# Two small TensorE products in a kernel's head computed as row sums on POOL and ScalarE

## What is computed

```python
def L0(x, y, weight, mask, bias):                 # first layer
    masked_w = weight * mask[None]
    w_bot = einsum('bg,got->bot', y, masked_w)
    return einsum('bnt,bot->bno', x, w_bot) + bias

def L1(x, w, W_base, b_base, As, Bs):             # second layer, low-rank experts
    out = einsum('btc,oc->bto', x, W_base) + b_base
    h = einsum('btc,erc->bter', x, As)
    return out + einsum('bter,eor,be->bto', h, Bs, w) * 2.0

x = x + L0(x, cond_8, ...)
x = x + L1(x, cond_8, ...)
x = x + L2(x, cond_8, ...)                        # shared MLP and two of eight routed MLPs
x = x + L3(x, cond_8, ...)                        # one of eight gated MLPs, with biases
```

## Time and profile before

| What | Value |
|---|---|
| Runs | 134.33, 134.73, 135.54 us, median 134.73 |
| The profiled execution | 134.23 us, its span 132.4 us |
| Granted TensorE clock, mean | 0.997 of full speed |
| Busy share of PE, DVE, ACT, POOL | 97%, 75%, 75%, 57% |
| Instructions | 3286 |

### The profile page before, as it was taken

One profiled execution on the slowest core, in us unless ns is written; L12 is line 12 of the kernel. 1 busy time (PEld: TensorE's weight loads), 2 busy tenths in 40 slices (PEclk: granted clock), 3 DMA queues, 4 the chain that ended last, 5 costly groups with the idle time before them and its releaser, 6 DMA issues.

```text
span 132.4 us, 3286 instructions
## 1 busy us (share of the span) xinstructions
PE 128.1 (97%) x930; PEld 120.0 (91%) x930; DVE 98.8 (75%) x192; ACT 99.2 (75%) x206; POOL 75.8 (57%) x90
## 2 busy tenths in 40 slices
PE   7999999999999999999999999999999999999990
PEld 5978888888888999999999999999999999999980
DVE  0699898797776777767967777767768676898791
ACT  3784799979945569787797877766866769989860
POOL 0238459979970037468496785963542544426790
PEclk9999999999999999999999999999999999999998
DMA  4999999999005946566765657756577565664216
GB/s 134 358 398 409 407 401 400 400 403 392 29 0 240 372 184 247 228 239 246 317 272 222 249 228 304 298 226 249 220 288 313 228 254 226 273 272 186 82 44 198
DMA packets 11490, 34.56 MB, mean 261 GB/s; under 512 B 1104, under 2 KB 2512, under 8 KB 11472
## 3 DMA queue, kind: packets, MB, share of 16 engines
q1 hardware_dynamic: 11184, 34.15, 65.8%
q10 hardware_dynamic: 288, 0.20, 0.5%
HBM read 12.32 MB, written 1.05 MB: 101 GB/s over the span
## 4 chain that ended last, share of the span: by engine, by line
PE 89%; ACT 3%; POOL 1%; issue 1%; DVE 1%; ACTq 1%; DVEq 0%; POOLq 0%
PE up L298 30%; PE acc L298 30%; PE gate L298 29%; ACT h_pair L619 1%; DVE x_res L979 1%; POOL x_lo L762 1%; POOL x_res L788 1%; ACT h_pair L692 1%; ACT h_act L683 1%; ACTq L224 0%; ACT h_act L672 0%; DVE h_pair L1010 0%; ACT dn_hi L637 0%; ACT out_part L661 0%; POOL dn_lo L756 0%
## 5 line engine op out<-in xcount | busy, mean ns | idle before, releaser
L756 POOL TENSOR_TENSOR dn_lo<-slabs,dn_hi 128x256 fp32r<-128x256 f32 x40 | 29.7, 742 | 39.0 <-ACT dn_hi L637 38.9
L613 ACT ACTIVATE h_act<-gate 128x512 f32<-128x512 f32 x48 | 28.8, 600 | 23.2 <-PE gate L298 21.1
L907 DVE TENSOR_TENSOR h_pair<-up,h_pair 128x512 fp32r<-128x512 f32 x55 | 37.6, 684 | 0.0
L917 DVE SCALAR_TENSOR_TENSOR up<-h_act,w_route,up 128x512 f32<-128x512 f32 x32 | 24.2, 756 | 16.9 <-PE up L298 16.7
L298 PE MATMUL gate<-x_hi,w_gu 128*128 128x256 f32 x160 | 33.9, 276 | 0.0
L298 PE MATMUL up<-x_hi,w_gu 128*128 128x256 f32 x158 | 33.4, 276 | 0.0
L619 ACT ACTIVATE h_pair<-up 128x512 fp32r<-128x512 f32 x55 | 32.9, 598 | 0.0
L298 PEld LDWEIGHTS gate<-x_hi,w_gu 128*128 128x128 f32 x160 | 27.1, 188 | 0.2
L298 PEld LDWEIGHTS up<-x_hi,w_gu 128*128 128x128 f32 x158 | 26.8, 188 | 0.0
L298 PE MATMUL acc<-h_pair,dn_hi 128*128 128x256 f32 x140 | 25.6, 276 | 0.0
L298 PE MATMUL gate<-x_lo,w_gu 128*128 128x256 f32 x80 | 22.1, 276 | 0.0
(11 more groups left out here) (125 smaller groups left out, 201.4 us busy)
## 6 DMA issues: line engine op xcount, KB each, us to landing
w_gu<-slabs SPq DMA_DIRECT2D x40, 512.0 KB, 3.1
slabs<-slabs_moe SPq DMA_DIRECT2D x8, 768.0 KB, 12.7
slabs<-slabs_l SPq DMA_DIRECT2D x4, 768.0 KB, 9.3
sh_raw<-slabs_shared SPq DMA_DIRECT2D x2, 384.0 KB, 5.0
x_res<-x_rest SPq DMA_DIRECT2D x1, 768.0 KB, 6.6
outT<-x_res SPq DMA_DIRECT2D x6, 128.0 KB, 2.0
slabs<-second_in SPq DMA_DIRECT2D x1, 320.0 KB, 3.1
slabs<-third_in SPq DMA_DIRECT2D x1, 256.0 KB, 3.8
```

The source lines that it names most:

```text
L613: nc.scalar.activation(h_act[:, u % 2, :], gate_ps[u % 2][:], ACT.Gelu_apprx_tanh).then_inc(act_done, 1)
L756: nc.gpsimd.tensor_tensor(dn_lo[:, q % W_SLOTS, :], slab_cols(at, DOWN_AT, 256), dn_hi[:, q % W_SLOTS, :].bitcast(F32), ALU.subtract).then ...
L907: V.tensor_tensor(h_lo[:, u % H_SLOTS, :], h_of(u), h_hi[:, u % H_SLOTS, :].bitcast(F32), ALU.subtract).then_inc(h_lo_done, 1)
L917: ins = V.scalar_tensor_tensor(h_of(u), h_act[:, k, :], weight, h_of(u), ALU.mult, ALU.mult)
```

## The change

The products As bias_l0 and (W_base) bias_l0 are no longer computed on PE. POOL multiplies each matrix elementwise with a row that repeats bias_l0 on all partitions, and ACT sums each product along its rows with the accumulator output of an Identity. So `lora_aT` isn't loaded any more, and W_base is loaded a second time, untransposed, with the repeated row beside it: `fourth_in` has four blocks of 128 columns where it had three. The identity's part of the constant, bias_l0 itself, is added to bias_l1 on POOL. PE keeps one product for the constant, line 358. On DVE the scaling of the product moves behind the two masks of batches 2 to 7, and `c_b` takes two per-partition operands, and waits for both sums and for POOL's.

```diff
-        fourth_sb = early(3, P)
+        fourth_sb = early(4, P)
...
-        w_baseT, ident, lora_aT = (fourth_sb[:, k, :] for k in range(3))
+        w_baseT, ident, w_base, bias_row = (fourth_sb[:, k, :] for k in range(4))
...
+        bias_terms = early(2, P)
...
+        a_bias, base_bias, bias_sum = (sb(n, [P, 1]) for n in ("a_bias", "base_bias", "bias_sum"))
...
             pe.wait_ge(bw_ready, 1)
             lora(gate_ps[0][:, 0:S], 0, 2)
-            pe.wait_ge(d_fourth, DMA)
-            mm(acc_ps[:, 512:512 + B], lora_aT, bias_l0.to_broadcast([P, B]), True, True).then_inc(a_bias_sum, 1)
             pe.wait_ge(bw_ready, 2)
...
             lora(up_ps[1][:, 0:S], 6, 2)
-            pe.wait_ge(base_ready, 1)
             pe.wait_ge(a_bias_ready, 1)
-            mm(acc_ps[:, 0:B], base_i[:], bias_l0.to_broadcast([P, B]), True, False)
-            mm(acc_ps[:, 0:B], lora_bT, a_bias_y[:], False, True).then_inc(c_sum, 1)
+            mm(acc_ps[:, 0:B], lora_bT, a_bias_y[:], True, True).then_inc(c_sum, 1)
...
             nc.scalar.activation(table_first[:, 0:1], cond_sb[:, 0, 0:1], ACT.Gelu_apprx_tanh)
+            act.wait_ge(term_ready, 1)
+            nc.scalar.activation(bias_terms[:, 0], bias_terms[:, 0], ACT.Identity, accum_out=a_bias[:]).then_inc(a_bias_sum, 1)
             round_shared(0)
+            act.wait_ge(term_ready, 2)
+            nc.scalar.activation(bias_terms[:, 1], bias_terms[:, 1], ACT.Identity, accum_out=base_bias[:]).then_inc(bias_sum_ready, 1)
             act.wait_ge(x2_first_sum, 1)
...
             nc.gpsimd.tensor_tensor(base_i[:], ident, w_baseT, ALU.add).then_inc(base_ready, 1)
+            pool.wait_ge(d_third, DMA)
+            nc.gpsimd.tensor_tensor(bias_terms[:, 0], lora_a, bias_row, ALU.mult).then_inc(term_ready, 1)
+            nc.gpsimd.tensor_tensor(bias_terms[:, 1], w_base, bias_row, ALU.mult).then_inc(term_ready, 1)
+            pool.wait_ge(d_first, DMA)
+            nc.gpsimd.tensor_tensor(bias_sum[:], bias_l0, bias_l1, ALU.add).then_inc(bias_sum_ready, 1)
             pool.wait_ge(hit_ready, 1)
...
-            dve.wait_ge(a_bias_sum, 1)
-            V.tensor_tensor(a_bias_y[:], acc_ps[:, 512:512 + B], cond_scaled[:], ALU.mult).then_inc(a_bias_ready, 1)
             mask_w0(0, 2, 6)
             mask_w0(1, 2, 6)
+            dve.wait_ge(a_bias_sum, 1)
+            V.tensor_scalar(a_bias_y[:], cond_scaled[:], a_bias[:], None, ALU.mult).then_inc(a_bias_ready, 1)
...
             dve.wait_ge(c_sum, 1)
-            V.tensor_scalar(c_b[:], acc_ps[:, 0:B], bias_l1, None, ALU.add).then_inc(acc_read, ACC_BIAS)
+            dve.wait_ge(bias_sum_ready, 2)
+            V.tensor_scalar(c_b[:], acc_ps[:, 0:B], base_bias[:], bias_sum[:], ALU.add, ALU.add).then_inc(acc_read, ACC_BIAS)
...
-    fourth = np.stack([base, np.eye(P, dtype=np.float32), as_.T], axis=1)
+    bias_row = np.broadcast_to(a(L0_cond_bias), (P, P))
+    fourth = np.stack([base, np.eye(P, dtype=np.float32), a(L1_cond_W_base), bias_row], axis=1)
```

More of the change, by code:

```diff
@@ L193, in build @@
         r1_first, m_first_sum, m_first = sem("r1_first"), sem("m_first_sum"), sem("m_first")
-        a_bias_sum, a_bias_ready, c_sum = sem("a_bias_sum"), sem("a_bias_ready"), sem("c_sum")
+        term_ready, a_bias_sum, a_bias_ready, c_sum, bias_sum_ready = (sem(n) for n in ("term_ready", "a_bias_sum", "a_bias_ready", "c_sum", "bias_sum_ready"))
         x2_first_sum, x2_sum, x2_ready, x2_hi_half, x2_hi, x2_lo = (
```

## The result

| | before | changed |
|---|---|---|
| Median | 134.77 us (22 runs) | 135.08 us (22 runs) |
| Ratio | 1 | 1.0033, 95% interval 1.0017 to 1.0049, or +0.44 us (+0.23 to +0.66) |
| Profiled execution, its span | 134.23 us, 132.4 us | 135.33 us, 133.3 us |

The changed kernel is slower by a third of a per cent, clear of noise but under the 1% that the forecast took as the limit of no change. One execution of each kernel, of 186.99 and of 138.02 us, lies far above all others and has no part in the ratio. The two profiled executions differ by 0.9 us of span, twice as much as the ratio says, so the trace of the changed kernel must be read with care.

The account below looks back on a forecast made before the run. TensorE bounds the kernel, its dense part starting when VectorE's `add_base(2)` ends. Removed products and DMA counted nothing; waiting for ScalarE's sums added 0.44: 134.73 + 0.44 = 135.2 us, bounds 135.06 to 135.58, range 134.5 to 136.0.

Parts of the forecast that it names:

- Only the head counts, one to one: Before 11.09 us: whatever the first shared product's start moves by, the end moves by; +0.44 us.
- The removed products are worth nothing: TensorE's head: two products, 0.29 us, lie ahead of VectorE-set waits and gain nothing, at most 0.29 us.
- ScalarE's price of a sum: ScalarE's row sum: 0.30 us plus a 0.20 read-out overlapping by 0.1; result after 0.40, next instruction after 0.30.
- rival C: ScalarE before the first sum: another function table load of 1.28 us, giving 136.4 us; chance 3%.
- D: ScalarE: handing out a sum costs more than a whole small instruction; 136.1 us at 0.85 us per sum; chance 5%.
- ScalarE's floor: Head: VectorE waits for the first sum behind its masks, `a_bias_y` at 8.67, `matrix(1)` load at 10.37; +0.44 us.
- The DMA: `fourth_in`: 64 KB more lands 0.18 us later, within 0.25 us of cover before VectorE needs `base_i`; counted as nothing.
- the sign that the forecast itself had named: `base_i` delaying VectorE's line 863 would show that the load's cover of 0.25 us was smaller.
- What the sum was made on: Head: start times taken from the one profiled execution of the kernel before, 134.23 us, with +0.44 us added to its span.
- The idle time of 0.2 to 0.5 us before `a_bias_y`: Sign of a right forecast: VectorE idle that long before `a_bias_y`, released by ScalarE.
- VectorE's small instructions: VectorE's head: `a_bias_y` takes 0.16 us, its successor starting 0.1 us later; `c_b` assumed as before.

Follow-up runs that it names:

- e6: The kernel before with `add_base(2)` moved ahead of `c_b` on VectorE and nothing else; ratio 1.0016 (0.9984 to 1.0048).
- e4: The changed kernel with each of ScalarE's two sums done twice; ratio 1.0077, +1.04 us over the kernel before.
- e7: The changed kernel with its four-block load split into two loads of 128 KB; ratio 1.0045, +0.60 us against the kernel before.
- e2: The kernel before without the two TensorE products and with no sums on ScalarE or POOL; ratio 1.0002, +0.03 us.
- e11: The changed kernel with `fourth_in` kept at 192 KB, POOL's second term using the transposed W_base; ratio 1.0022, +0.30 us against the kernel before.
- e8: The kernel before with `fourth_in` grown by three unread blocks, 384 instead of 192 KB; ratio 1.0053, +0.71 us.
- e5: The changed kernel with `add_base(2)` moved ahead of `c_b` on VectorE; ratio 1.0022, +0.30 us against the kernel before.
- e1: The kernel before with `fourth_in` grown by one unread block, 64 KB more; ratio 1.0043, +0.58 us.

## Why the prediction was right, and where it wasn't

The forecast of +0.44 us is what the ratio gives, but the agreement of the two numbers is partly luck, as the points show.

- **Only the head counts, one to one.** Right: 121.5 to 121.6 us behind the first shared load in eleven of fourteen traces, both of the changed kernel among them. The other three lose time behind that load: e6 waits once more for `sh_lo`, e4 has the lower clock, and e7 loses 0.9 us at the very end for a reason that wasn't found.
- **The removed products are worth nothing.** Right as far as e2 shows: +0.03 us, and its trace has TensorE waiting for VectorE in their place, the stated reason.
- **ScalarE's price of a sum.** Right: 0.29 us and a read-out of 0.19 overlapping by 0.09, 0.39 us to the result, against 0.30, 0.20 and 0.40 worked out. The read-out is an instruction of its own. The Trainium skill ("VectorE: DVE Perf Modes", section "Two Vector instructions with no wait between them") counts an operation that writes out its accumulator as two instructions on VectorE, and on ScalarE these traces have two as well. Neither rival C (no table load was added) nor D came.
- **ScalarE's floor.** Right as a mechanism: e11 has `a_bias_y` at 8.76 (8.67 forecast) and `matrix(1)` at 10.56 (10.37), the rest of the difference being the 0.10 later table load and the dearer instructions of the last point. e4 has one sum more in front of each of the two, and `a_bias_y` at 8.99; in e7, with the start of the head free, VectorE waits for each of the two sums.
- **The DMA.** Wrong, the step that failed: the forecast had the landing 0.18 us later, 0.25 us of cover, and counted it as nothing. The landing came 0.5 to 0.7 us later in five of six traces with the four-block load, and 0.4 per block in e8. That uses up the cover, the sign that the forecast itself had named: `base_i` delays the first base addition in the traces of e5 and e8. e1 measured +0.2 to +0.95 us for the larger load alone, more than this delay accounts for. Bytes over a mean rate gave 0.18 us where 0.5 to 0.7 came; why a transfer in the midst of a queue lands so much later isn't shown.
- **How they add up.** The forecast had one cost and no second one. There were two, each about as large as the whole (e1 +0.58, e11 +0.30, with wide intervals), and they don't seem to add: the changed kernel measures +0.36 and +0.44. The reading that fits is that both are floors under the same start, 0.13 us apart in the trace of e5, so that missing the one cost little because the other was already there. That the number came out as forecast in spite of a cost left out is luck. How the +0.44 divides among them can't be told from these runs.
- **What the sum was made on.** The trace of before was one of the executions with an early TensorE. The sum took its times as the kernel's. For executions with a late TensorE, like the profiled one of the changed kernel, ScalarE's sums cost nothing and only VectorE's 0.12 us is left. The idle time of 0.2 to 0.5 us before `a_bias_y` that was to show the step right isn't in either trace of the changed kernel (0 and 0.1 us); it is in e11's, 0.48 us.
- **VectorE's small instructions.** The last term mis-sized: `a_bias_y` and `c_b` with per-partition operands take 0.22 and 0.27 us with the successor after 0.13 and 0.19, against 0.16 and 0.22 and about 0.10 and 0.13 assumed. Against the kernel before, that makes the 0.12.

## What to carry to other kernels

Moving small products off the busiest engine pays only if they were what the next stage waited for; ask first who the busy engine itself waits for, and here it was VectorE's addition. When work goes to an idle engine, look at its absolute time of arrival: an engine that is idle on average can still be busy with a table load just when the result is wanted, and its result then puts a floor under executions that would have been fast. A changed load in the first microseconds can be an edit to the critical path, however few bytes it adds, and so can one more DMA in the queue; and where single executions differ by more than the effect, compare the distributions of runs and differences within one trace, not two traces.

## What the hardware showed that wasn't expected

- The moment at which TensorE's early products go from a step of 0.21 to 0.11 us varies by over a microsecond between executions of kernels with nearly the same start, with the recorded clock at 1.00 throughout. That it makes most of the spread of the kernel before is a guess, as there is one trace of each variant.
- The landing of the first load varies by 0.33 us (3.34 to 3.67), and ScalarE's table load, 3.43 to 3.50 us behind it, varies with it.
- 64 KB more in the fourth of SP's queued transfers came with a landing 0.5 to 0.7 us later in five traces and not later in one (e4); a fourth transfer of 128 KB landed at 5.6, 5.7 and 6.3 us, so chance has a part in this.
- After two waits of TensorE of 1.45 and 0.82 us, the granted clock went to 0.50 for some 3 us (e4); after 1.07 and 0.99 us (e7) it didn't.
